# Two token layers: one subtraction per unit moved from GpSimd to the vector engine

## The reference, cut to what matters

```python
g = jnp.einsum('th,ehi->tei', x, w_gate)
u = jnp.einsum('th,ehi->tei', x, w_up)
eo = jnp.einsum('tei,eih->teh', jax.nn.silu(g) * u, w_down)
routed = jnp.einsum('te,teh->th', cw, eo)
shared = jax.nn.silu(x @ shared_w_gate) * (x @ shared_w_up) @ shared_w_down
out = routed + shared + ANCHOR_ALPHA * anchor
```

## Time and profile before

| | |
|---|---|
| median of three runs | 1696.62 us |
| profiled execution, its own time | 1697.44 us |
| span of its profile | 1695.7 us |
| PE busy (share of the span), matmuls | 1386.6 us (82%), 9096 |
| DVE busy, instructions | 1173.5 us (69%), 2854 |
| ACT busy, instructions | 795.0 us (47%), 1482 |
| GpSimd busy, instructions | 717.4 us (42%), 905 |
| subtractions of lf on GpSimd | 84, 111.2 us, mean 1326 ns |
| subtractions of lh on GpSimd | 84, 111.4 us, mean 1328 ns |
| mean granted clock of PE | 0.915 of 2.4 GHz |

### The profile page before, as it was taken

The page is one execution under the profiler, slowest core; times in us unless marked ns, Lnnn a source line. Parts: engine busy times, 40 slices in busy tenths (PEclk is TensorE's granted clock), DMA queues, the critical chain, the costliest instruction groups (busy, mean ns, idle before and its releaser), DMA issues. The chain is left out here.

```text
span 1695.7 us, 26855 instructions
## 1 busy us (share of the span) xinstructions
PE 1386.6 (82%) x9096; PEld 942.8 (56%) x9096; DVE 1173.5 (69%) x2854; ACT 795.0 (47%) x1482; POOL 717.4 (42%) x905
## 2 busy tenths in 40 slices
PE   4799999947996549988699898989996477389997
PEld 3333333235884327873377676767883277266886
DVE  5777777466555774557589798778777754769776
ACT  2277767631113122217787675445554311164554
POOL 3833341025642028620078687046663051006665
PEclk9699999968998759998899999899997599699999
DMA  1244240000100100100011110554440000074453
GB/s 41 62 115 130 85 142 11 1 26 13 37 25 12 25 0 26 37 20 12 22 38 44 32 44 26 196 125 124 134 125 7 1 1 1 13 225 120 134 131 106
DMA packets 77882, 104.76 MB, mean 62 GB/s; under 512 B 25184, under 2 KB 43120, under 8 KB 77232
## 3 DMA queue, kind: packets, MB, share of 16 engines
q1 hardware_dynamic: 77760, 103.23, 21.3%
HBM read 92.81 MB, written 10.39 MB: 61 GB/s over the span
## 5 line engine op out<-in xcount | busy, mean ns | idle before, releaser
L526 DVE CUSTOM_DVE_ANT_1 la_neg<-bank,la_table 128x512 f32<-128x512 f32 x256 | 166.4, 688 | 44.8 <-PE bank L617 44.2
L1673 POOL TENSOR_TENSOR lh_h_low<-lh_hidden,lh_h_high 128x512 fp32r<-128x512 f32 x84 | 111.4, 1328 | 158.3 <-ACT lh_h_high L1706 157.2
L1389 DVE TENSOR_TENSOR_SCAN le_h<-le_keep,bank 128x512 f32<-128x512 f32 x128 | 152.4, 1212 | 27.0 <-issue 15.5
L1471 PEld LDWEIGHTS bank<-le_diag,le_dtxT 128*128 128x128 f32 x1024 | 126.4, 192 | 58.2 <-ACT le_diag L1308 32.8
L1673 POOL TENSOR_TENSOR lf_h_low<-lf_hidden,lf_h_high 128x512 fp32r<-128x512 f32 x84 | 111.2, 1326 | 108.5 <-ACT lf_h_high L1706 108.3
L1471 PE MATMUL bank<-le_diag,le_dtxT 128*128 128x128 f32 x1024 | 133.4, 279 | 21.2 <-ACT le_diag L1308 12.0
L453 ACT ACTIVATE la_probT<-bank 128x512 f32<-128x512 f32 x256 | 135.6, 605 | 12.9 <-PE bank L636 10.9
L1243 POOL TENSOR_TENSOR le_hc<-le_h,le_c_row 128x512 f32<-128x512 f32 x64 | 81.5, 1274 | 127.9 <-DVE le_h L1389 88.9
L1696 ACT ACTIVATE bank<-bank 128x512 f32<-128x512 f32 x144 | 83.7, 582 | 63.4 <-PE bank L1861 61.7
L1308 ACT ACTIVATE le_diag<-ident,le_bT 128x128 f32<-128x128 f32 x256 | 81.0, 388 | 44.7 <-PE bank L1471 44.7
L48 PE MATMUL bank<-ident 128*128 128x512 bf16 x150 | 43.9, 459 | 62.3 <-DVEq L830 40.4
(11 more groups left out here) (569 smaller groups left out, 3558.5 us busy)
## 6 DMA issues: line engine op xcount, KB each, us to landing
lf_weight<-lf_scratch SPq DMA_DIRECT2D x128, 128.0 KB, 3.0
lh_weight<-lh_scratch SPq DMA_DIRECT2D x128, 128.0 KB, 3.1
le_c_row<-le_scratch SPq DMA_DIRECT2D x32, 256.0 KB, 3.0
la_table<-la_scratch SPq DMA_DIRECT2D x4, 1792.0 KB, 7.1
lf_weight<-lf_scratch SPq DMA_DIRECT2D x64, 64.0 KB, 2.2
lh_weight<-lh_scratch SPq DMA_DIRECT2D x64, 64.0 KB, 2.2
la_bias_parts<-la_scratch_parts SPq DMA_DIRECT2D x12, 248.0 KB, 6.3
lb_w1s<-in_L_ffn_w_dram SPq DMA_DIRECT2D x8, 256.0 KB, 2.8
```

The costliest lines, as they stand in the source:

```text
L526: dve.tensor_tensor_reduce(out=neg[:, u % 2, :].rearrange("p (c i) -> p c i", i=P), in0=k.bank[u % RING1][:].rearrange("p (c i) -> p c i", ...
L1389: dve.tensor_tensor_scan(h[:, i, :], keep[:, i, :], k.bank[4 + q % 2][:], 0.0, ALU.mult, ALU.add).then_inc(scanned, 1)
L1471: last = pe.matmul(k.bank[4 + q % 2][:, j * P:(j + 1) * P], dtxT[:, (g * G2 + bb) * TPB + j, c, :], diag[:, d % DIAGS, j, :], start=True, ...
L1673: pool.tensor_tensor(h_low[:, u % RING, :], hidden[:, u % RING, :], h_high[:, u % RING, :].bitcast(F32), ALU.subtract)\
```

## The change

The subtraction leaves GpSimd's list, which is then empty in the loop, and goes into DVE's. It stands behind the hidden product of the next unit and ahead of the step of the second routing: hidden product `u`, subtraction `u - 1`, step, gate product `u + 1`. The last one, of unit 83, comes after the loop, ahead of the last `add_acc`. It keeps its two waits, for the unit's `h_high` and, from the fifth unit on, for the down product that last read the buffer of `h_low`. The wait of the hidden product for the subtraction four units before it goes. The tiles, shapes, formats and all other engines' lists stay as they are.

```diff
         @block.gpsimd
         def _(pool):
             k.clear_past()
-            for u in range(U):
-                pool.wait_ge(h_high_ready, u + 1)
-                if u >= RING:
-                    pool.wait_ge(down_done, u - RING + 1)
-                pool.tensor_tensor(h_low[:, u % RING, :], hidden[:, u % RING, :], h_high[:, u % RING, :].bitcast(F32), ALU.subtract)\
-                    .then_inc(h_low_ready, 1)
...
+            def remainder(u):
+                dve.wait_ge(h_high_ready, u + 1)
+                if u >= RING:
+                    dve.wait_ge(down_done, u - RING + 1)
+                dve.tensor_tensor(h_low[:, u % RING, :], hidden[:, u % RING, :], h_high[:, u % RING, :].bitcast(F32), ALU.subtract)\
+                   .then_inc(h_low_ready, 1)
+
...
-                if u >= RING:
-                    dve.wait_ge(h_low_ready, u - RING + 1)
                 if t < LATE:
                     dve.wait_ge(up_done, v + 1)
                 dve.tensor_tensor(hidden[:, u % RING, :], sl, up, ALU.mult).then_inc(hidden_ready, 1)
+                if u:
+                    remainder(u - 1)
                 if u < SECOND_DUE:
                     next(second, None)
...
+            remainder(U - 1)
             add_acc(B - 1)
```

## The result

The changed kernel takes 1712.04 us (median of five runs, 1709.07 to 1712.54), the kernel before 1696.62 us (five runs, 1691.15 to 1698.86). The ratio is 1.0083 with a 95% interval of 1.0056 to 1.0110: slower by 15.4 us. The profiled execution took 1712.54 us, 15.1 us more than the one before.

A forecast was written before the change was run, and what follows sets the result against it. DVE was taken to bound each loop's first stretch and PE the second. Terms of 8.0 + 0.6 in lf and 9.1 + 0.3 in lh gave +18.0 on 1697.4, so 1715 us, own range 1707 to 1723, overall 1704 to 1736.

The forecast's parts named there:

- Price of a subtraction: On DVE, one subtraction takes 0.60 us between starts, as it needs nothing of the instruction before it.
- Rival A: DVE starts each subtraction only once the hidden product is out, 0.73 instead of 0.61: 20 us more, 1735; chance 0.15.
- First stretch: Units 0 to 21 of each loop: 22 subtractions add 13.2 us on DVE; net +8.0 in lf, +9.1 in lh.
- Second stretch: From unit 23's gate product to the last remainder: DVE bound by a hair, 118.3 us; net +0.6 lf, +0.3 lh.
- What the second stretch of lh had been: Length before the change in lh, from unit 23's start to the last remainder: 118.0 us, so net +0.3.
- The new waits: DVE's subtraction waits for its unit's rounding and the down product four units before; both should be over when issued.
- Rival B: TensorE's clock falls at all six turns and sometimes in first stretches; eight waits of 2.27, 18 us: 1733; chance 0.12.
- Rival C: PE lags behind GpSimd's contention in the second stretch; removing it gives up to 6 us a layer: about 1697; chance 0.11.

The follow-up runs named there:

- half width: Changed kernel with DVE's subtractions over half the columns from the fifth unit on, the rest left as an older unit made it; 1699.99 us.
- the first stretch on GpSimd: Changed kernel with the subtractions of units 0 to 21 back on GpSimd and those of 22 to 83 on DVE; 1697.29 us.
- the second stretch on GpSimd: Changed kernel with the subtractions of units 22 to 83 back on GpSimd and those of 0 to 21 on DVE; 1711.63 us.

## Why the prediction was right

The forecast was 1715 us, +18.0 on the profiled execution; it came to +15.1. Step by step:

- **Price of a subtraction, 0.60:** right, by the starts in the timeline. Rival A, the same instruction held back, was made on purpose and costs the 20 us it was priced at (24 in the medians, 19.8 in the loops).
- **First stretch, +8.0 and +9.1:** the mechanism was right, the size is +7.4 and +8.2. With 22 x 0.60 = 13.2 added, 5.8 came back in lf and 5.0 in lh, against 5.15 and 4.1: the smaller routing steps that the sum left out were hit by GpSimd as well. What DVE's instructions in the first stretch took beside GpSimd over what they take in the changed kernel comes to 4.8 in lf and 5.0 in lh, and lf's wait of 1.05 for a weight is gone.
- **Second stretch, 118.3 us:** 118.10 and 118.11, in the parts that were worked out: 116.0 to the start of hidden product 83 against 116.2, and a tail of 2.1. DVE became the bound by about 2 us, half width against full, where 0.6 a chunk, 1.8 over the stretch, had been worked out, and the shorter tail gave 1.4 back.
- **What the second stretch of lh had been, 118.0:** wrong, the term of the sum that was mis-sized. The chain of waits showed one subtraction from 1684.36, and I took its end for the last one's. GpSimd's own timeline of the kernel before shows two in a row:

```profile
1684.36 2.64 POOL L1673 TENSOR_TENSOR lh_h_low<-lh_hidden,lh_h_high 128x512 fp32r<-128x512 f32 x2 [0.28 <-ACT lh_h_high L1706]
```

  So that stretch had been 1684.36 + 2.64 - 1567.77 = 119.2, and its net is -1.1, not +0.3. (The chain shows the second subtraction's time as 1.25 us of GpSimd's sequencer, POOLq.) With it the sum is 7.4 + 0.4 + 8.2 - 1.1 = 14.9. Of the 119.2, 1.5 us go with the fall of TensorE's clock at the first turn in that profile: hidden product 83 started 115.8 us after unit 23's gate product there, and 114.2 in lf, where the clock stood at 1.00.
- **The new waits:** none of them held DVE. Its groups in the second stretch show 0.1 us of idle time ahead of all 62 subtractions, and none ahead of the gate products.
- **Rival B, the clock:** it did fall in the first stretches, to a mean of 0.94 and 0.97, and single pauses of PE reached 1.7 us where 0.7 had been expected, but no time was lost: DVE, not PE, sets the pace there. In the second it stood at 1.00. Where the clock did fall in a second stretch, that stretch was longer: by 1.5 us in lh before, and by 1.5 in lf with the first stretch on GpSimd. The changed kernel's pause at the first turn, 1.6 us instead of 2.5, was followed by none.
- **Rival C, contention as the whole story:** the early hidden products did shorten by 1 us each, as C had it, but the second stretch gained nothing by it, since PE does not lag behind them. With the second stretch on GpSimd they are back at 1688 ns, and hidden product 83 starts 113.6 us after unit 23's gate product; at half width there is no contention, DVE waits 11.0 us for silus, and it starts after 114.2. What contention costs in the second stretch lies in DVE's idle time. What it cost in the first, about 5 us, was in the sum.

## What to carry to other kernels

What an operation costs on another engine differs from stretch to stretch: here 22 subtractions cost 15.6 us over both layers, and the other 62 nothing that the time shows. Ask in each stretch which engine ends last, and multiply by the distance between starts there, not by the duration. What an idle GpSimd gives back to DVE counts only where DVE is the bound. And take the end of a stretch from the engine's own timeline; the chain of waits can list the last instruction under another name.

## What the runs showed that I had not expected

A DVE instruction that reads SBUF alone and meets GpSimd's subtraction does not run at a lower rate: if it starts while the subtraction runs, it is held until that is over, and does its own work then. In the traces with both engines at work, such an instruction (TENSOR_TENSOR, SCALAR_TENSOR_TENSOR, TENSOR_SCALAR or COPY in the rows) ended no earlier than 0.02 us behind the subtraction at 8 columns, 0.14 at 128 and 0.54 at 512. So its duration tells how early it met the subtraction: 8 columns took 1.15 us instead of 0.17, 512 columns up to 1.79 instead of 0.69. The slow product of the earlier trace rows, which ends at 1170.20, shows it beside GpSimd's timeline of the kernel before, where the subtraction ends at 1169.65:

```profile
1168.03 1.62 POOL L1673 TENSOR_TENSOR lf_h_low<-lf_hidden,lf_h_high 128x512 fp32r<-128x512 f32 x1 [0.28 <-ACT lf_h_high L1706]
```

The hold goes both ways: that subtraction started while a gate product on two SBUF tiles ran, which ends at 1168.48, and itself ended 1.17 after it, with 1.62 us instead of 1.29. No subtraction that started while a TENSOR_TENSOR, SCALAR_TENSOR_TENSOR or TENSOR_SCALAR on SBUF alone ran ended less than 1.13 us after it. Hidden products of late units, which read a PSUM bank, took 0.69 us (686 to 692 ns) in every run. The routing's searches (MAX8, MATCH_REPLACE8) read SBUF alone and were not held: they took 0.17 to 0.19 us within a subtraction. The GPSIMD Engine Reference of the Trainium skill (section: Key points) names contention with DVE instructions that have two inputs in SBUF; the traces agree, and they give its size. Of the instructions with one input, a TENSOR_SCALAR of 8 columns was held as well, with 1.10 us instead of 0.17.

TensorE's clock fell twice in the first stretch of lf in the changed kernel: after a pause of 3.10 us at 1107.40, and after one of only 1.66 us, below (at 1.2 GHz the matmuls start 0.43 apart). After a third pause of 1.62 us, at 1136.20, it stayed at 2.4 GHz. DVE waited for PE after none of them.

```profile
1118.04 0.80 PE L1923 MATMUL bank<-lf_h_low,lf_wd_high 128*128 128x512 f32 x1 [1.66 <-DVE lf_h_low L1823]
1118.63 0.63 PE L1861 MATMUL bank<-lf_x_high,lf_wg_high 128*128 128x512 f32 x1
1119.06 0.63 PE L1862 MATMUL bank<-lf_x_low,lf_wg_high 128*128 128x512 f32 x1
```
